# Decoder kernel, first mixture of experts: gathers issued ahead of scatters, three routing steps a slot later, the last tile's third matrix in a free block

## What is computed

```
x = _layernorm(x + _L0_attn_ref(x, ...))
x = _layernorm(x + _L0_xattn_ref(x, ctx_768, ...))
x = _layernorm(x + _L0_ffn_ref(x, L0_ffn_Wg, L0_ffn_W1, L0_ffn_W2, L0_ffn_W3))
```

## Time and profile before

| | us |
|---|---|
| median of three runs | 1141.53 |
| the profiled execution | 1150.01 |
| its span, first to last instruction | 1148.3 |
| PE busy in the span | 1013.1 (88%) |
| DVE busy | 617.3 (54%) |
| ACT busy | 425.2 (37%) |
| POOL busy | 255.9 (22%) |
| mean granted clock of TensorE, 1 being full | 0.968 |

### The profile page before, as it was taken

How to read it: one execution, slowest core, us unless ns; L and a number is a source line. 1 busy time by engine, 2 the same in 40 slices (tenths; PEclk the granted TensorE clock), 3 DMA queues, 4 the chain that set the end, 5 groups by cost and what they waited for, 6 DMA issues and landing times.

```text
span 1148.3 us, 20834 instructions
## 1 busy us (share of the span) xinstructions
PE 1013.1 (88%) x8628; PEld 723.1 (63%) x8628; DVE 617.3 (54%) x1398; ACT 425.2 (37%) x557; POOL 255.9 (22%) x282
## 2 busy tenths in 40 slices
PE   6889889889998898999998798989888987986887
PEld 3666566566565798997445465756556574753656
DVE  2653753753867463333334845665574759755333
ACT  1533533533513445555541244152406323340212
POOL 0310310310210223333332130231103111202642
PEclk9999999999988898999999899999999999997999
DMA  6014313213201971111112000200010010005427
GB/s 186 1 42 149 109 42 125 69 42 121 73 1 32 370 237 37 47 47 47 47 43 92 1 5 2 83 2 6 16 59 2 6 37 1 2 1 152 151 88 233
DMA packets 64238, 80.50 MB, mean 70 GB/s; under 512 B 12736, under 2 KB 57681, under 8 KB 63121
## 3 DMA queue, kind: packets, MB, share of 16 engines
q1 hardware_dynamic: 53392, 61.15, 16.1%
q0 software_dynamic: 5664, 15.47, 4.2%
q10 hardware_dynamic: 5088, 2.56, 0.9%
HBM read 46.13 MB, written 33.03 MB: 69 GB/s over the span
## 4 chain that ended last, share of the span: by engine, by line
PE 44%; issue 21%; DVE 16%; ACT 12%; SPq 2%; DMA 2%; POOL 2%; another core or an unknown queue 1%; ACTq 0%; DVEq 0%; POOLq 0%
PE ps L1511 8%; DVE sb_arena L865 6%; ACT sb_arena L642 6%; PE ps L1647 5%; PE ps L1669 3%; PE ps L1717 3%; PE ps L1772 3%; DVE sb_arena L869 3%; PE ps L1619 2%; PE ps L1983 2%; DVE ps L886 2%; PE ps L1555 1%; SPq L433 1%; PE ps L1998 1%
## 5 line engine op out<-in xcount | busy, mean ns | idle before, releaser
L642 ACT ACTIVATE sb_arena<-ps 77x2048 f32<-77x2048 f32 (+1 forms) x64 | 116.7, 1880 | 28.2 <-PE ps L1601 27.0
L1377 POOL TENSOR_TENSOR sb_arena<-sb_arena,sb_neghalf 128x2 f32<-128x2 f32 x40 | 28.7, 719 | 398.1 <-DVE sb_arena L831 398.1
L1511 PE MATMUL ps<-sb_arena,sb_wreg 128*128 128x256 f32 (+1 forms) x512 | 109.0, 361 | 6.8 <-issue 3.8
L1846 PE MATMUL ps<-sb_arena 128*128 128x128 f32 x800 | 104.4, 287 | 2.4 <-ACT sb_arena L750 2.1
L1846 PEld LDWEIGHTS ps<-sb_arena 128*128 128x128 f32 x800 | 101.2, 203 | 4.5 <-ACT sb_arena L750 2.8
L1511 PEld LDWEIGHTS ps<-sb_arena,sb_wreg 128*128 128x128 f32 (+1 forms) x512 | 88.0, 193 | 23.3 <-issue 8.3
L1619 PE MATMUL ps<-sb_arena 32*77 32x256 f32 (+1 forms) x1024 | 79.4, 428 | 25.3 <-ACT sb_arena L642 12.7
L750 ACT ACTIVATE sb_arena<-sb_arena 128x1024 f32 x72 | 76.0, 1056 | 17.1 <-issue 13.1
L1619 PEld LDWEIGHTS ps<-sb_arena 32*77 32x77 f32 (+1 forms) x1024 | 45.0, 179 | 45.8 <-ACT sb_arena L642 23.7
L865 DVE TENSOR_REDUCE sb_arena<-ps 128x8 f32<-128x2048 f32 x32 | 71.1, 2285 | 3.5 <-PE ps L1575 3.5
L1452 POOL DMA_INDIRECT outs<-sb_arena,sb_idx x36 | 36.3, 1010 | 145.6 <-ACT sb_arena L740 145.6
(11 more groups left out here) (285 smaller groups left out, 1890.4 us busy)
## 6 DMA issues: line engine op xcount, KB each, us to landing
sb_arena<-in_m_w SPq DMA_DIRECT2D x8, 1536.0 KB, 10.7
sent<-sb_xres SPq DMA_DIRECT2D x32, 256.0 KB
sb_arena<-outs SPq DMA_DIRECT2D x16, 512.0 KB, 6.3
outs<-sb_zeros SPq DMA_DIRECT2D x4, 1664.0 KB, 9.8
sent<-sb_zeros SPq DMA_DIRECT2D x2, 2560.0 KB, 13.7
sb_arena<-in_m_w SPq DMA_DIRECT2D x16, 256.0 KB
early<-sb_xres SPq DMA_DIRECT2D x12, 256.0 KB, 2.9
sb_arena<-in_xT SPq DMA_DIRECT2D x8, 256.0 KB, 3.4
```

The source lines that it names most:

```text
L642: nc.scalar.activation(dst, src, ACT.Exp).then_inc(S(f"h_PT{p}"), 1)
L1511: ins = mm(dst[:, m * cols:(m + 1) * cols], wt[0:rows, k, m * P:(m + 1) * P], src[0:rows, k, 0:cols], start=(k == 0), stop=(k == KC - 1))
L1846: ins = mm(to[:, m * P:(m + 1) * P], w[:, k, m * P:(m + 1) * P], slots0[j % 2].xT[:, k, :], start=(k == 0), stop=(k == KC - 1))
```

## The change

Four edits, all in the first mixture:

1. POOL issues gather j+4 ahead of its wait for output j and of scatter j, not behind them.
2. `LATE_INDEX` goes from 8 to 9 and `LATE_WEIGHTS` from 9 to 10: `index` and `weigh` on DVE and `router(1)` on ACT stand one step later. `place_late` on PE stands at the end of step 5, not 4.
3. ACT's `picks(2, 2)`, the copy to `raw`, stands at the end of step 7, not 8. Its readers on PE stay at the end of step 8.
4. For the last tile ACT copies W3 to the first third of `work`, where W1 was, and does so as soon as W1's matmuls of that tile are done, ahead of the output of tile 34. PE reads it there.

```diff
-LATE_CHOOSE, ..., LATE_RAW, LATE_INDEX, LATE_WEIGHTS = 0, 2, 3, 5, 6, 8, 8, 9
+LATE_CHOOSE, ..., LATE_RAW, LATE_INDEX, LATE_WEIGHTS = 0, 2, 3, 5, 6, 8, 9, 10
...
             def weights0(j, part, used, signal):
+                last = j + 1 == TILES0 and part == 2
                 if j < E:
                     act.wait_ge(S(f"landed{j}"), 16)
-                if j:
+                if last:
+                    act.wait_ge(S("t_u"), TILES0)
+                elif j:
                     act.wait_ge(S(used), j)
...
+                to = WORDS * WORK + (0 if last else 1024 * part)
...
                 if j + 1 < TILES0:
                     weights0(j + 1, 0, "t_u", "t_c1")
+                if j + 1 == TILES0:
+                    weights0(j, 2, "t_y", "t_c3")
                 if j:
                     outputs0(j - 1)
+                if 0 < j < TILES0 - 1:
                     weights0(j, 2, "t_y", "t_c3")
-                if j == LATE_RAW:
+                if j == LATE_RAW - 1:
                     picks(2, 2)
...
             for j in range(TILES0):
+                if j + XBUFS < TILES0:
+                    gather0(j + XBUFS)
                 pool.wait_ge(S("t_ys"), j + 1)
                 g.indirect_dma_start(outs0[:, :], ..., y0t[j % XBUFS], None).then_inc(...)
-                if j + XBUFS < TILES0:
-                    gather0(j + XBUFS)
-                else:
+                if j + XBUFS >= TILES0:
                     unread(j % XBUFS)
...
             def output_halves(j, blk):
+                at = 0 if j + 1 == TILES0 else 2 * KC * FH
...
-                if j == LATE_HOTS + 1:
+                if j == LATE_HOTS + 2:
                     place_late(0)
```

More of the change, by code:

```diff
@@ L54 @@
 HOTS = 2 * EARLY
-LATE_CHOOSE, LATE_RANK, LATE_HOTS, LATE_TABLE, LATE_QUANTA, LATE_RAW, LATE_INDEX, LATE_WEIGHTS = 0, 2, 3, 5, 6, 8, 8, 9
+LATE_CHOOSE, LATE_RANK, LATE_HOTS, LATE_TABLE, LATE_QUANTA, LATE_RAW, LATE_INDEX, LATE_WEIGHTS = 0, 2, 3, 5, 6, 8, 9, 10
 FAR = 128 * P
@@ L749, in weights0 @@
                 blk = act.value_load(copied_of(j), min_val=0, max_val=max(BLOCKS))
-                nc.scalar.activation(arena[:, WORDS * WORK + 1024 * part:WORDS * WORK + 1024 * (part + 1)],
-                                     arena[:, bass.ds(blk * WORDS + 1024 * part, 1024)], ACT.Copy).then_inc(S(signal), 1)
+                to = WORDS * WORK + (0 if last else 1024 * part)
+                nc.scalar.activation(arena[:, to:to + 1024], arena[:, bass.ds(blk * WORDS + 1024 * part, 1024)], ACT.Copy).then_inc(S(signal), 1)
             act.wait_ge(S("store"), B)
@@ L1863, in block_at, with weights_of @@
                 return pe.value_load(block_q[0:1, first:first + 1], min_val=0, max_val=max(BLOCKS))
-            def weights_of(c, blk, at, size):
-                at_work = WORDS * WORK + at
+            def weights_of(c, blk, at, size, at_half):
+                at_work = WORDS * WORK + at_half
                 return arena[:, at_work:at_work + size] if c else arena[:, bass.ds(blk * WORDS + at, size)]
@@ L1873, in hidden_halves @@
                         rows = slice(QROWS * c, QROWS * (c + 1))
-                        ins = mm(to[rows, :], slots0[j % 2].xT[:, k, rows], weights_of(c, blk, at + FH * k, FH), start=(k == 0), stop=(k == KC - 1),
+                        ins = mm(to[rows, :], slots0[j % 2].xT[:, k, rows], weights_of(c, blk, at + FH * k, FH, at + FH * k), start=(k == 0), stop=(k == KC - 1),
                                  skip_group_check=True)
@@ L1892, in output_halves @@
                         rows = slice(QROWS * c, QROWS * (c + 1))
-                        ins = mm(bank(1, 3)[rows, 0:D], slots0[p].hT[:, m, rows], weights_of(c, blk, 2 * KC * FH + D * m, D), start=(m == 0),
+                        ins = mm(bank(1, 3)[rows, 0:D], slots0[p].hT[:, m, rows], weights_of(c, blk, 2 * KC * FH + D * m, D, at + D * m), start=(m == 0),
                                  stop=(m == MC - 1), skip_group_check=True)
```

## The result

Twenty runs of each kernel: before 1144.08 us (1140.96 to 1151.63), changed 1135.93 us (1131.08 to 1140.35). The ratio of changed to before is 0.9911 with a 95% interval of 0.9897 to 0.9926: faster by 0.9%, 8.5 to 11.8 us; the two medians lie 8.15 us apart. The forecast was 1130.5 us with a range of 1126.5 to 1137.0. The profiled execution took 1137.67 us, 12.3 less than the one before.

The account below looks back on a forecast made before the run. The prediction took PE to bound the loop, so only its stalls and the slow clock behind them count. Terms 4.9 + 5.2 + 0.9 = 11.0 us off 1141.5 gave 1130.5 us, range 1126.5 to 1137.

Parts of the forecast that it names:

- harmless gathers: Rival: gathers are not late outside the profile, or not for their queue place; gain 6.1 to 6.6 us, 1135; chance 0.08.
- forecast 4.25 us at step 3 and 4.9 up to step 8: First mixture: step 3 falls from 9.77 to 5.52 us; with 0.45 moved out and 0.2 of gather wait, 4.9.
- DVE is late next: Steps 5 to 8: DVE's untouched 14.09 us chain of tables makes PE wait about 1.05 us at step 8.
- forecast 5.2 us: Steps 8 and 9: earlier `raw` cuts 17.22 us to 12.02, 2.0 of it the wait and the rest the clock.
- the 0.45 of `place_late`: PE delay by spreading the late tables, moved from ahead of the DVE chain's start to behind it: 0.45 us.
- forecast 0.9: Last tile: earlier W3 copy lets PE start at 601.1 instead of 602.02, then released by DVE's copy: 0.9 us.
- the two for the clock: Slow matmuls behind PE's gather wait in step 3 and its `raw` wait, claimed to return to full clock: 1.8 and 2.9 us.
- the new wait at step 8: PE's wait for DVE, 0.28 growing to 1.05 us; clock cost taken as none, possibly 1.5 to 2.9 us.
- The clock did not fall at step 8: Rival: the longer wait at step 8 lowers the clock, giving back 1.5 to 2.9 us, 1132 to 1133.4; chance 0.17.
- Block 2 was late for PE: Rival: gather 4 ahead of the loads of blocks 2 to 7 delays step 2; up to 4.1 us lost, 1134.6; chance 0.05.
- The kernel did not get slower: Rival: the clock falls at step 8 or earlier and stays low for steps; four such steps give 1152.6; chance 0.03.
- signs of error: Block 2 wait in step 1 or 2, clock under 1 behind step 8, another gather wait, second layer over 2 us longer.

Follow-up runs that it names:

- edit 1 alone: The kernel before with only the gathers issued ahead of the scatters, against the kernel before: ratio 0.9951 (0.9932 to 0.9971).
- the second profile: The changed kernel run again with nothing altered, against the kernel before: ratio 0.9913 (0.9882 to 0.9943), span 1134.0 us.

## Why the prediction was right, and what in it was off

The direction, the mechanism and the range held. The stated point was 5.4 us too fast: 1135.93 us lies 1.1 inside the upper end of the range, outside the forecast's own 1128 to 1133, and near the 1135 of a rival (harmless gathers) that edit 1 alone then ruled out. That the time was inside the range owes something to its width; the waits and steps of the profile are what bear the mechanism out.

**Edit 1, forecast 4.25 us at step 3 and 4.9 up to step 8.** Measured against the same profile: from W1 of step 2 to W1 of step 8 39.74 us before (391.50 to 431.24) and 34.79 now (392.21 to 427.00), 4.95 less. The handover to VectorE came as worked out: a wait of 0.93 us at step 8 where 1.05 was forecast. That one sentence of the working, "DVE is late next", kept the forecast from counting the other 0.9 us of gather wait. From the transposes of tile 3 to those of tile 9, over all four profiles of before, edits 1 and 2 take off 4.95, 5.55, 3.38 and 3.44 us (mean 4.3).

**Edit 3, forecast 5.2 us.** Against the same profile 5.4: W1 of step 9 starts 6.15 us behind that of step 8, as forecast 6.5 (the readers themselves take 0.66 at full clock, and I had read their 0.98 from a stretch at the low one).

**Edit 2, forecast 0 beside the 0.45 of `place_late`.** Measured 0.54.

**Edit 4, forecast 0.9.** Measured 0.87.

**The mis-sized terms are the two for the clock**, 1.8 us in step 3 and 2.9 (with the slow readers 3.2) behind `raw`. They were read from a single execution and booked in full. Behind `raw`, edit 3 takes off 5.4, 2.3, 3.9 and 3.9 us against the four profiles of before, 3.9 in the mean and not 5.2. In step 3 the clock was low in the first of the four only. Over the four the kernel before loses 8.2 us against the changed one in the loop (78.4 - 70.2), where the forecast had 10.1 and the first profile 10.4; with 0.9 for the tail that is 9.1 us. The timed runs say 8.5 to 11.8, an interval that holds the forecast's 11.0 as well, so it is the profiles and not the timing that show these terms too large. The rule of the expectations, a wait of 2 us or more costs the clock that falls behind it, fails as a price for each such wait: two in ten were free of it. The prediction named the uncertainty of such a fall for the new wait at step 8, but not for the ones it took away.

**The other part of the miss is the level.** The 1141.53 us from which 11.0 was taken was a median of three runs at the fast end; over twenty the kernel before has 1144.08. This is 2.55 of the 5.4 us; the remaining 2.85 are the 11.0 against the 8.15 between the medians. The prediction also took it that profiled executions take 8.5 us longer. The later ones do not bear that out: the changed kernel's took 1137.67, 1.7 above its median, and the three of before, on another chip, 1142.90, 1146.52 and 1143.84. The first one, of 1150.01, was a long execution, as two of the twenty timed ones were too (1150.10 and 1151.63), and the terms were read from it. In the result's list of twenty runs of the changed kernel the fastest (1131.08 us) has a mean granted clock of 0.980 and the slowest (1140.35) of 0.965.

**The rivals.** The clock did not fall at step 8: 1.00 in every profile with a wait of 0.9 to 1.4 us there. The gathers were not harmless: edit 1 alone has a timed ratio of 0.9951. Block 2 was late for PE in one of the six profiles with edit 1, by 0.5 us (edit 1 alone, above); in the changed kernel's first profile ScalarE waits 1.5 us for it instead of 1.14, and PE for nothing. The kernel did not get slower.

**What I had set as signs of error.** The part behind tile 35 was to keep its length within 2 us. It took 555.8 us (1135.9 - 580.13) against 558.5 (1148.3 - 589.82), 1.8 less beyond edit 4's 0.9, and 554.4 in the second profile. The kernel before itself has 558.5, 555.3, 556.7 and 554.4 over its four, so this is the spread of that part, and no effect of the change is shown in it. That, and the long loop of the first profile of before, is why the two first profiles differ by 12.4 us and the timed runs by 10.

## What to carry to other kernels

When a stall is followed by matmuls at a lower clock, count the stall in full and the clock only as often as it falls: profile the kernel before two or three times more, for here one profile overstated the loop's gain by 2.2 us. Before booking the second of two waits on one engine, follow the other engine's chain across both, because it may set the later point anyway. Work whose result is read only after a loop may stand behind it, in a wait that is there already: here this took 1.5 us off the loop in the profile, a gain that the timing does not settle.

## What the runs showed of the hardware

- The same wait of 2.0 us on TensorE, at the same place of the same instructions, was followed by the full clock in two profiled executions and by a lower one in four (step of 8.47 us against 9.20 to 10.48). Of the ten waits of 1.99 to 2.57 us in the loops of seven profiles eight had a low clock at or behind them, and every one of these profiles had one; six profiles without such a wait had 1.00 over the loop. Waits of 0.9 to 1.4 us at step 8 and of 1.7 ahead of the last matmuls were followed by 1.00 in every profile.
- Filling the two waits with matmuls whose results are not used kept the clock at 1.00 in its profile, yet won 1.5 us or nothing in the timed runs.
- With the DMA engines full or nearly so (a share of 0.9 to 1.1 in the windows up to 420 us), the gathers of one kernel were late by different amounts in four executions: PE waited 2.4, 1.4, 1.4 and 1.5 us for tile 4, 0.9, 2.1, 0.8 and 0.4 for tile 7, and for tile 5 in three of the four (0.8 to 1.2). With each gather from the fifth on issued a step or more earlier, PE waited for none of these in six profiles; a wait of 0.5 to 0.7 us for the first tile's rows, whose gather the change does not move, stays in three of them.
- From the transposes of tile 14 to those of tile 35 every profile has 121.84 or 121.85 us: a stretch in which PE never waits repeats to a hundredth, and all spread lies outside it.
